# Decoder block with a mixture of experts: a new order behind the scan, earlier loads for the last group, and a second buffer for expert outputs

## The chip, the cores and the metric

One core of a Trainium2 chip runs the whole program. The metric is the device time of one execution in microseconds; the number given for a kernel is the median of several executions.

## What is computed

Eight rows (batch entries) of 256 positions with 256 features pass through a decoder block in float32. Each sublayer is added to its input and layer-normed:

```python
x = _layernorm(x + mamba_2_layers(x))      # selective scan, 512 channels x 64 states, 256 steps, twice
x = _layernorm(x + cross_attention(ctx, ctx, x))
# mixture of experts: 8 experts, hidden 1024, the best two of each position
gate_probs = softmax(xf @ gate_w.T); topk_scores, topk_idx = top_k(gate_probs, 2)
h   = relu(einsum('td,ehd->teh', xf, w1) + b1)
out = einsum('ted,te->td', einsum('teh,edh->ted', h, w2) + b2, combine)
x = _layernorm(x + out)
```

`combine` is zero but for the two chosen experts of a position, so only those two need be computed for it.

## The kernel before

**The scan.** There are 16 jobs (8 rows x 2 layers, `JOBS`, layer 1 of a row after layer 0 of the next row) and 64 states in each: 1024 steps (`STEPS`). A step is a scan over 128x1024 on VectorE (h), fed by a decay from ScalarE (dA), a product or a turned tile in PSUM (psX), and followed by a product on GpSimd (hC) and transposes that add up on TensorE (psY).

**Everything else is planned beside it.** `Schedule` builds three chains of small tasks: chain 0 is the work of the scan's own jobs (projections, convolution, residual and norm of a finished row), chain 1 is the attention and the gate of a row (`tasks_row`: x1_turn, q, score, prob, p_turn, av, o, resid2, norm2, x2_turn, logit, top, weights, count, place, list, send, b2, spill), chain 2 the experts (`tasks_experts`). A task has an engine, a nominal duration and what it needs. `fill` puts tasks between the scan's steps; `run_off` orders what is left behind the last step (`plan.tail`). Its rule: among the first `WINDOW` = 24 tasks of each chain whose needs are placed, the one with the earliest start is placed next, ties going to the lower chain. The result is one list, and every engine walks through its own pieces of that list in that order, waiting on semaphores. SyncE (SP) walks through it too: it issues the DMAs of the pieces, and a wait in one piece holds the pieces behind it.

**The experts.** The rows form four groups of two (`GROUPS`). When the last row of a group has been gated, `list` works out which expert each of the group's 15 tiles of 128 slots belongs to; four indirect DMAs per row (`send`, on GpSimd) put its positions into `x_slots` by slot. Tile t (0 to 59; 45 to 59 are the last group's, `TILE0[-2]` is 45) then runs:

- `tile_in`: SP waits and loads 128 rows of x and the expert's b1 (`load_tile`); for the first tile of a group it first waits until all sends of the group have landed, and behind x it asks for weights (`load_quarters`);
- `x_turn` (TensorE, transpose), `xg_copy` (ScalarE), 8 `hid` pieces (TensorE) with two `relu` (ScalarE), 8 `out` pieces (TensorE), `y_copy` into the single buffer yg (ScalarE), and `tile_out` (SP stores yg into `y_slots`).

An expert's weights come in four quarters, each a `w_up` and a `w_down` load of 256 KB. There are 3 slots of each during the scan and 9 behind it (`NW`, `NT`; the freed buffers of dA and h serve, so the trace calls these loads dA and h). `load_quarters` asks in turn for up and down loads until 9 quarters stand ahead of the pieces used; it is called at every second `hid` or `out` piece of the list, and it waits until the slot it fills is free. When the 15 tiles of a group are stored, each row fetches its two results per position (`fetch`, four indirect DMAs a row on GpSimd), adds them to its loaded accumulator (`acc_load`, `blend`), is normed (`bn3`, `rstd`, `norm3`) and stored; SP's store stands in the list at the place of `norm3`.

There is one `y_slots` tensor: the first `tile_out` of a group waits until the rows of the group before have been fetched. `x_slots` has two buffers. All these tensors are cleared during the first scan steps (`clear`, 24 DMAs of 512 KB, one every second step).

At the end of the scan in the kernel before, tiles 43 and 44 (third group), the fetches of rows 4 and 5, all of row 7 behind the scan, and the last group's 15 tiles are still to be done.

Of the kernel before, what the change touches and what calls it, by code (L numbers as in the profile page):

```python
# [20 lines left out]
P = 128  # L21
# [240 lines left out]

def tasks_experts(g):
    out = []
    for t in range(TILE0[g], TILE0[g + 1]):
        out.append(task("tile_in", t, 0, "DMA", 6000, ("list", GROUPS[g][-1], 0), ("sent", GROUPS[g][-1], 0),
                        *((("x_turn", t - 1, 0),) if t else ()), *((("y_copy", t - 2, 0),) if t > 1 else ())))
# [8 lines left out]
        for half in range(2):  # L276
            for i in range(4):
# [5 lines left out]
                     *((("fetched", GROUPS[g - 1][-1], 0),) if g and t == TILE0[g] else ()))]  # L283
# [20 lines left out]
class Schedule:  # L304
# [55 lines left out]
    def run_off(self, where, small, sums):  # L360
        banks = {"G": small, "M": sums}
        while any(self.chains):
            ready = []
            for rank, chain in enumerate(self.chains):
                for t in chain[:WINDOW]:
                    at, k = self.start(t, banks)
                    if at is not None:
                        ready.append((at, rank, chain, t, k))
            at, _, chain, t, k = min(ready, key=lambda r: r[:2])
            self.place(chain, t, at, k, where)  # L370
# [105 lines left out]
def decoder_block(nc, io, out):  # L476
    plan = Schedule()
    turn = plan.turn
    with ExitStack() as ctx:
# [127 lines left out]
        y_slots = nc.dram_tensor("y_slots", [SLOTS, D], F32, kind="Internal").ap()  # L607
# [37 lines left out]
        CLEARS = 3 * SLOTS * D // (P * KL * 2 * D)  # L645
# [8 lines left out]
        def _(eng):  # L654
# [8 lines left out]
            def clear(at):  # L663
                tensor, part = (*x_slots, y_slots)[at // (CLEARS // 3)], at % (CLEARS // 3)
                n = P * KL * 2
                on.wait_ge(got_cleared, 1)
                eng.dma_start(tensor[part * n:(part + 1) * n, :].rearrange("(p a) d -> p (a d)", p=P),
                              got[:, :, :, :].rearrange("p c k d -> p (c k d)")).then_inc(cleared, 16)
# [16 lines left out]
            def load_quarters(t):  # L685
                listed_to[0] = max(listed_to[0], PAIRS * TILE0[group_of_tile(t) + 1])
                missing = True
                while missing:
                    missing = False
                    for name, load in (("hid", load_up), ("out", load_down)):  # L690
                        if loaded[name] < min(used[name] + depth[0], listed_to[0]):
# [4 lines left out]
            def load_tile(t):  # L696
                g = group_of_tile(t)
                if t == TILE0[g]:
# [10 lines left out]
                if t == TILE0[g]:  # L709
                    load_quarters(t)  # L710

            def store_tile(t):
# [3 lines left out]
                for b in GROUPS[g - 1] if g else ():  # L716
                    on.wait_ge(fetched[b], 16 * 4)
                on.wait_ge(cleared, 16 * CLEARS)
                eng.dma_start(y_slots[bass.DynSlice(tile_combo(t) * P, P), :], yg[:, :]).then_inc(y_tile_out, 16)
# [110 lines left out]
        def _(eng):  # L830
# [13 lines left out]
            def small_work(pieces):  # L844
                for name, n, part in pieces:
# [25 lines left out]
                    elif name == "fetch":  # L871
# [6 lines left out]
                        eng.indirect_dma_start(got_of[n][:, tc, k, :], None, y_slots, bass.IndirectOffsetOnAxis(slot_of[:, n, k, tc:tc + 1], 0),  # L878
# [868 lines left out]
```

## Time and profile before

| | us |
|---|---|
| median of 3 runs (3365.19 to 3372.42) | 3367.84 |
| the profiled execution | 3358.99 |
| its span | 3357.3 |

| engine | busy us | share |
|---|---|---|
| PE (TensorE) | 2737.2 | 82% |
| DVE (VectorE) | 3050.3 | 91% |
| ACT (ScalarE) | 2743.0 | 82% |
| POOL (GpSimd) | 2658.3 | 79% |

DMA moved 319 MB, 95 GB/s over the span. In the slices of the page VectorE is at nine tenths or more nearly up to the last scan step at 3134 us and idle behind it; the DMA's rate goes up to three times its mean there. So a share over the whole span tells only of the scan; the 223 us behind it have to be read by themselves. Times in the rows are microseconds from the start of the span.

### The profile page before, as it was taken

The page shows a single profiled execution, that of the slowest core. Times are in us where ns is not written, and L with a number is a line of the kernel's source. Part 1 is how long each engine was busy: PE and PEld are TensorE (multiplying, and loading weights), DVE is VectorE, ACT ScalarE, POOL GpSimd, SP SyncE. Part 2 cuts the span into 40 slices and gives each one's busy share as a digit, 9 for nine tenths or more (in the row PEclk, how much of TensorE's full clock was granted, in tenths as well). Part 3 has the DMA queues.
Part 4 walks back from the last instruction along what each step waited for, and adds up shares of the span by engine and source line. Part 5 has one row for each costly group of instructions (what it writes and reads, how often), then busy time and mean ns, then how long its engine had stood idle before and what let it go on. Part 6 is the DMA issues. An engine that isn't in the chain of part 4 may idle for free.

```text
span 3357.3 us, 54622 instructions
## 1 busy us (share of the span) xinstructions
PE 2737.2 (82%) x19466; PEld 2406.5 (72%) x19466; DVE 3050.3 (91%) x2211; ACT 2743.0 (82%) x6424; POOL 2658.3 (79%) x1289
## 2 busy tenths in 40 slices
PE   6878787888878877888888888878888777888876
PEld 4767776777767766777776777767777666778665
DVE  6999999999999999999999999999999999999500
ACT  7889898898978898898989888897998869888422
POOL 5989998898989788887888788797887878877401
PEclk7999999999999999999999998999999979999988
DMA  3241111111111113223331333313232122433485
GB/s 100 96 147 58 45 54 52 45 55 45 49 60 45 46 45 119 89 77 117 102 115 60 114 123 112 129 68 125 96 102 93 50 86 82 149 122 129 133 284 187
DMA packets 151747, 319.34 MB, mean 95 GB/s; under 512 B 28570, under 2 KB 44963, under 8 KB 151092
## 3 DMA queue, kind: packets, MB, share of 16 engines
q1 hardware_dynamic: 147522, 305.08, 27.7%
q0 software_dynamic: 3072, 8.39, 0.7%
q8 instruction: 155, 2.54, 0.3%
q10 hardware_dynamic: 882, 2.38, 0.2%
q14 instruction: 116, 0.95, 0.1%
HBM read 285.90 MB, written 29.88 MB: 94 GB/s over the span
## 4 chain that ended last, share of the span: by engine, by line
DVE 28%; issue 28%; ACT 15%; PE 14%; POOL 13%; DMA 1%; SPq 1%; POOLq 0%; DVEq 0%
DVE h L1146 15%; POOL hC L916 12%; DVE psX L1136 10%; ACT dA L1114 7%; PE psY L1452 3%; PE psG L1399 3%; ACT xs L1085 3%; PE psX L1436 2%; PE psX L1434 1%; PE psX L1399 1%; PE psG L1478 1%; PE psX L1478 1%; ACT gT L965 1%; ACT diag_b L1083 1%; DVE gT L1161 0%
## 5 line engine op out<-in xcount | busy, mean ns | idle before, releaser
L916 POOL TENSOR_TENSOR hC<-h,cb 128x1024 f32<-128x1024 f32 x1024 | 2404.8, 2369 | 493.6 <-DVE h L1146 487.7
L1146 DVE TENSOR_TENSOR_SCAN h<-dA,psX 128x1024 f32<-128x1024 f32 (+1 forms) x1115 | 2305.6, 2102 | 70.1 <-PE psX L1436 34.1
L1114 ACT ACTIVATE dA<-dt,negA 128x255 f32<-128x255 f32 x4096 | 1716.5, 502 | 105.2 <-DVE h L1146 103.0
L1452 PE MATMUL psY<-ident,hC 128*128 128x128 f32 x8192 | 1123.5, 283 | 47.4 <-DVE gT L1161 37.3
L1452 PEld LDWEIGHTS psY<-ident,hC 128*128 128x128 f32 x8192 | 978.1, 146 | 61.7 <-DVE gT L1161 41.0
L1136 DVE TENSOR_TENSOR psX<-dtu,psX 128x1024 f32<-128x1024 f32 x513 | 619.6, 1208 | 9.5 <-PE psX L1423 9.3
L1436 PE MATMUL psX<-ident,xs 128*128 128x128 f32 x3280 | 465.0, 288 | 158.8 <-ACT xs L1085 78.2
L1085 ACT ACTIVATE xs<-dtuT,bT 128x512 f32<-128x512 f32 x820 | 545.9, 718 | 12.7 <-PE psX L1436 12.4
L1436 PEld LDWEIGHTS psX<-ident,xs 128*128 128x128 f32 x3280 | 387.2, 148 | 234.9 <-ACT xs L1085 151.4
L1423 PE MATMUL psX<-ident,bT 128*128 128x128 f32 x1026 | 217.3, 295 | 194.8 <-DVE h L1146 192.1
L1423 PEld LDWEIGHTS psX<-ident,bT 128*128 128x128 f32 x1026 | 117.4, 141 | 299.5 <-DVE h L1146 280.4
L1434 PE MATMUL psX<-diag_b,dtuT 128*128 128x128 f32 x1616 | 215.5, 289 | 63.3 <-DVE h L1146 38.9
L1434 PEld LDWEIGHTS psX<-diag_b,dtuT 128*128 128x128 f32 x1616 | 199.8, 201 | 84.0 <-issue 48.4
L1399 PE MATMUL psG<-xgT,w_up 128*128 128x128 f32 x1440 | 202.9, 285 | 12.4 <-DMA w_up<-in_w_exp 5.4
L1399 PEld LDWEIGHTS psG<-xgT,w_up 128*128 128x128 f32 x1440 | 186.9, 200 | 23.4 <-DMA w_up<-in_w_exp 6.9
L1478 PE MATMUL psG<-w_down,hid 128*128 128x256 f32 x720 | 193.5, 392 | 6.7 <-ACT hid L1066 4.7
L1066 ACT ACTIVATE hid<-psG,b_tile 128x128 f32<-128x128 f32 x388 | 109.3, 364 | 56.5 <-PE psG L1399 56.4
L1478 PEld LDWEIGHTS psG<-w_down,hid 128*128 128x128 f32 x720 | 127.9, 195 | 26.5 <-ACT hid L1066 8.2
L1358 DVE SCALAR_TENSOR_TENSOR acc<-got,slot_weight,acc 128x256 f32<-128x256 f32 x28 | 14.7, 543 | 144.4 <-DMA got<-y_slots,slot_of 124.7
L878 POOL DMA_INDIRECT got<-y_slots,slot_of x28 | 29.1, 1041 | 126.4 <-DMA y_slots<-yg 120.7
L1399 PE MATMUL psG<-xin,w_in 128*128 128x256 f32 x256 | 68.7, 399 | 8.8 <-DMA conv_w<-in_conv 6.2
L1083 ACT ACTIVATE diag_b<-ident,bT 128x128 f32<-128x128 f32 x202 | 69.3, 393 | 3.9 <-PE psX L1434 3.9
(206 smaller groups left out, 1992.7 us busy)
## 6 DMA issues: line engine op xcount, KB each, us to landing
cb<-c_dram SPq DMA_DIRECT2D x256, 512.0 KB
w_up<-in_w_exp SPq DMA_DIRECT2D x196, 256.0 KB, 3.0
w_down<-in_w_exp SPq DMA_DIRECT2D x196, 256.0 KB
dA<-in_w_exp SPq DMA_DIRECT2D x44, 256.0 KB, 4.4
h<-in_w_exp SPq DMA_DIRECT2D x44, 256.0 KB, 5.0
x_slots<-got SPq DMA_DIRECT2D x16, 512.0 KB, 5.3
xg<-x_slots SPq DMA_DIRECT2D x60, 128.0 KB, 2.7
y_slots<-yg SPq DMA_DIRECT2D x60, 128.0 KB
```

Source lines behind the costliest of these rows:

```text
L916: eng.tensor_tensor(hC[i % NHC][:, :, :], h[i % NH][:, :, :], cw.to_broadcast([P, KI, L]), ALU.mult).then_inc(times_c, 1)
L1066: made = eng.activation(hid[part][:, i, :], bank[k][:, i * P:(i + 1) * P], ACT.Relu, bias=b1_tile[n % 2][:, c:c + 1])
L1085: made = eng.activation(xs[:, tc, :], dtuT[n % 2][:, tc, :], ACT.Identity, scale=bT[n % 2][:, tc, s:s + 1])
L1114: made = eng.activation(dA[j % NA][:, c, 1:L], dt[n % 2][:, c, 1:L], ACT.Exp, scale=negA[:, JOBS[n][0], c, s:s + 1])
L1136: eng.tensor_tensor(x[:, :, :], dtu[n % 2][:, :, :], x[:, KI - 1:KI, :].to_broadcast([P, KI, L]), ALU.mult).then_inc(times_b, 1)
L1146: made = eng.tensor_tensor_scan(h[i % NH][:, part, :].rearrange("p c t -> p (c t)"), dA[i % NA][:, part, :].rearrange("p c t -> p (c t)"), ...
L1399: made = eng.matmul(dst, lhs, rhs, start=begin and i == 0, stop=end and i == len(terms) - 1)
L1423: made = eng.transpose(psX[i % 2][:, KI - 1, tc * P:(tc + 1) * P], bT[n % 2][:, tc, s:s + 1].to_broadcast([P, P]), ident[:, :])
L1434: made = eng.matmul(to, dtuT[i // S % 2][:, tc, c * P:(c + 1) * P], diag_b[:, tc, :], start=True, stop=True)
L1436: made = eng.transpose(to, xs[:, tc, c * P:(c + 1) * P], ident[:, :])
L1452: made = eng.matmul(psY[:, tc, c * P:(c + 1) * P], hC[i % NHC][:, c, tc * P:(tc + 1) * P], ident[:, :], start=s == 0 and c == 0, stop=s == ...
L1478: made = eng.matmul(bank[k][:, 0:D], hid[half][:, i, :], w_down[slot][:, i % 2, :], start=half == i == 0, stop=half == 1 and i == 3, skip_ ...
```

## The change

Five edits:

1. `run_off` looks at 48 tasks of each chain instead of 24, and orders PE and ACT tasks by their start plus 1500 ns for each rank of their chain (0, 1500, 3000); DMA, DVE and POOL tasks go by their plain start.
2. For the last group's tiles `tile_in` needs, in the plan, the x_turn and the second relu of the tile two before, in place of the x_turn of the tile before and the y_copy of the tile two before. The waits of `load_tile` itself are the same.
3. At the last group's first tile the weights of that tile alone (4 quarters, 8 loads) are asked for ahead of the wait for the sends; the call behind the load of x is dropped for this group.
4. `y_slots` has two buffers, used in turn; the first `tile_out` of a group waits for the fetches of the group before the last one, in the plan and in the code.
5. The clearing has 32 DMAs in place of 24.

```diff
+def tile_before(t):
+    if t >= TILE0[-2]:
+        return ("x_turn", t - 2, 0), ("relu", t - 2, 1)
+    return (*((("x_turn", t - 1, 0),) if t else ()), *((("y_copy", t - 2, 0),) if t > 1 else ()))
...
         out.append(task("tile_in", t, 0, "DMA", 6000, ("list", GROUPS[g][-1], 0), ("sent", GROUPS[g][-1], 0),
-                        *((("x_turn", t - 1, 0),) if t else ()), *((("y_copy", t - 2, 0),) if t > 1 else ())))
+                        *tile_before(t)))
...
                 task("tile_out", t, 0, "DMA", 2500, ("y_copy", t, 0),
-                     *((("fetched", GROUPS[g - 1][-1], 0),) if g and t == TILE0[g] else ()))]
+                     *((("fetched", GROUPS[g - 2][-1], 0),) if g > 1 and t == TILE0[g] else ()))]
...
-                for t in chain[:WINDOW]:
+                for t in chain[:2 * WINDOW]:
                     at, k = self.start(t, banks)
                     if at is not None:
-                        ready.append((at, rank, chain, t, k))
-            at, _, chain, t, k = min(ready, key=lambda r: r[:2])
+                        ready.append((at + (1500 * rank if t.eng in ("PE", "ACT") else 0), rank, chain, t, at, k))
+            _, _, chain, t, at, k = min(ready, key=lambda r: r[:2])
             self.place(chain, t, at, k, where)
...
-        CLEARS = 3 * SLOTS * D // (P * KL * 2 * D)
+        CLEARS = 4 * SLOTS * D // (P * KL * 2 * D)
...
-            def load_quarters(t):
+            def load_quarters(t, alone=False):
...
-                        if loaded[name] < min(used[name] + depth[0], listed_to[0]):
+                        if loaded[name] < min(used[name] + depth[0], PAIRS * (t + 1) if alone else listed_to[0]):
...
             def load_tile(t):
                 g = group_of_tile(t)
+                if t == TILE0[-2]:
+                    load_quarters(t, alone=True)
                 if t == TILE0[g]:
                     for b in GROUPS[g]:
                         on.wait_ge(sent[b], 16 * 4)
...
-                if t == TILE0[g]:
+                if t == TILE0[g] and t < TILE0[-2]:
                     load_quarters(t)
...
-                for b in GROUPS[g - 1] if g else ():
+                for b in GROUPS[g - 2] if g > 1 else ():
                     on.wait_ge(fetched[b], 16 * 4)
                 on.wait_ge(cleared, 16 * CLEARS)
-                eng.dma_start(y_slots[bass.DynSlice(tile_combo(t) * P, P), :], yg[:, :]).then_inc(y_tile_out, 16)
+                eng.dma_start(y_slots[g % 2][bass.DynSlice(tile_combo(t) * P, P), :], yg[:, :]).then_inc(y_tile_out, 16)
```

## Rows read from the trace of the kernel before

**Rows 1.** Stretches: us, PE, PEld, DVE, ACT, POOL busy (instructions), PE clock, DMA share, GB/s.
```profile
3150.00:3200.00 50.00, 29.53 (x148) 23.40 (x146) 15.95 (x65) 9.72 (x30) 14.33 (x15) 0.76 0.33 105
3200.00:3250.00 50.00, 41.70 (x239) 37.31 (x239) 3.98 (x11) 14.25 (x48) 0.72 (x1) 0.87 0.88 298
3250.00:3300.00 50.00, 46.82 (x310) 42.38 (x309) 0.00 (x0) 17.63 (x60) 0.00 (x0) 1.00 0.94 294
```

**Rows 2.** Timeline, row 7 behind the scan, in order of its chain: start, us, engine, line.
```profile
3142.40 1.04 PE L1558 MATMUL psX<-ident,gT 128*128 128x128 f32 x8
...
3155.69 0.47 ACT L939 ACTIVATE qT<-psX,b_att 128x256 f32<-128x256 f32 x1
3156.41 1.89 PE L1399 MATMUL psG<-kT,qT 128*128 128x256 f32 x8
3160.57 0.62 DVE L1263 TENSOR_SCALAR prob<-prob,small 128x256 f32<-128x256 f32 x2
3161.82 0.60 PE L1466 MATMUL psX<-ident,prob 128*128 128x128 f32 x4
3162.59 0.61 ACT L936 ACTIVATE x1T<-psX 128x512 f32<-128x512 f32 x1
3163.60 1.89 PE L1399 MATMUL psX<-x1T,vv 128*128 128x256 f32 x8
...
3185.08 0.17 DVE L1329 CAST slot_of<-small 128x4 int32<-128x4 f32 x1
```

**Rows 3.** Chain of waits that ended last, around the sends: start, us, what.
```profile
3190.05 2.39 DMA x_slots<-x,slot_of
...
3206.35 6.86 DMA xg<-x_slots
```

**Rows 4.** Timeline of SP's queue: start, us until issued, line, DMA.
```profile
3193.64 0.36 SPq L707 DMA_DIRECT2D xg<-x_slots  x1
...
3221.74 0.36 SPq L719 DMA_DIRECT2D y_slots<-yg  x1
```

**Rows 5.** Timeline, tiles 45 to 47, PE and ACT.
```profile
3196.70 0.69 PE L1655 MATMUL psX<-ident,xg 128*128 128x128 f32 x2 [9.67 <-DMA xg<-x_slots]
3199.44 2.05 PE L1399 MATMUL psG<-xgT,dA 128*128 128x128 f32 x8 [2.05 <-DMA dA<-in_w_exp]
3213.26 0.69 PE L1655 MATMUL psG<-ident,xg 128*128 128x128 f32 x2 [3.97 <-DMA xg<-x_slots]
3214.43 6.42 PE L1399 MATMUL psX<-xgT,dA 128*128 128x128 f32 x32 [0.47 <-ACT xgT L1054]
3220.69 3.62 PE L1478 MATMUL psG<-h,hid 128*128 128x256 f32 x16
3225.96 0.38 ACT L1073 ACTIVATE yg<-psG 128x256 f32<-128x256 f32 x1 [3.93 <-DMA y_slots<-yg]
3235.90 0.38 ACT L1073 ACTIVATE yg<-psX 128x256 f32<-128x256 f32 x1 [2.32 <-PE psX L1478]
```

**Rows 6.** The chain of waits in a later tile, and ACT's copy of the last one (timeline).
```profile
3248.49 3.47 PE psG L1478 x16
3251.98 0.26 ACT yg L1073
3252.26 0.39 ACT xgT L1054
...
3332.41 0.38 ACT L1073 ACTIVATE yg<-psX 128x256 f32<-128x256 f32 x1 [2.31 <-PE psX L1478]
```

**Rows 7.** Stretches of PE alone: us, PE busy (instructions), PE clock, DMA share, GB/s.
```profile
3206.00:3210.00 4.00, 3.29 (x16) 1.00 1.05 405
...
3216.00:3218.00 2.00, 2.00 (x12) 0.50 0.00 0
```

**Rows 8.** Stretches of the scan, with and without clears: columns as in rows 1.
```profile
100.00:400.00 300.00, 236.56 (x1846) 210.32 (x1846) 294.10 (x157) 263.72 (x616) 271.03 (x123) 0.98 0.28 92
400.00:700.00 300.00, 247.32 (x1844) 220.79 (x1845) 286.72 (x163) 262.68 (x609) 263.59 (x123) 0.95 0.14 50
```

More of the change, by code:

```diff
@@ L606, in decoder_block @@
         x_slots = [nc.dram_tensor(f"x_slots{i}", [SLOTS, D], F32, kind="Internal").ap() for i in range(2)]
-        y_slots = nc.dram_tensor("y_slots", [SLOTS, D], F32, kind="Internal").ap()
+        y_slots = [nc.dram_tensor(f"y_slots{i}", [SLOTS, D], F32, kind="Internal").ap() for i in range(2)]
         kept = nc.dram_tensor("kept", [ROWS, P, KL, D], F32, kind="Internal").ap()
@@ L663, in clear @@
             def clear(at):
-                tensor, part = (*x_slots, y_slots)[at // (CLEARS // 3)], at % (CLEARS // 3)
+                tensor, part = (*x_slots, *y_slots)[at // (CLEARS // 4)], at % (CLEARS // 4)
                 n = P * KL * 2
@@ L877, in small_work @@
                             on.wait_ge(blended, KL * n)
-                        eng.indirect_dma_start(got_of[n][:, tc, k, :], None, y_slots, bass.IndirectOffsetOnAxis(slot_of[:, n, k, tc:tc + 1], 0),
+                        eng.indirect_dma_start(got_of[n][:, tc, k, :], None, y_slots[GROUP_OF[n] % 2], bass.IndirectOffsetOnAxis(slot_of[:, n, k, tc:tc + 1], 0),
                                                bounds_check=SLOTS - 1, oob_is_err=False).then_inc(fetched[n], 16)
```

## Prediction

> **What bounds the kernel now.** I read the busy shares first, then the stretches behind the scan, then the chain of waits and the timelines of that part. The shares are the scan's: VectorE is the bound up to 3134 us, and nothing of the change enters a scan step but the clearing and small shifts of the plan. Behind the scan the stretches [rows 1] show two stages. Between 3150 and 3200 us no engine is the bound: TensorE is busy 29.5 of 50 us and DMA a third; it is a chain of small dependent steps of row 7, from the turn of its gated scan at 3142.40 to its slots at 3185.25 (3185.08 + 0.17) [rows 2]: 42.9 us. From 3200 us TensorE is the bound (41.7, then 46.8 of 50 us busy), with DMA busy 0.88 and 0.94 beside it. But that share is not a full queue: with the weights of 9 quarters asked for at once the same engines moved 405 GB/s [rows 7], against 294 in the steady stage [rows 1]. So there is room for an earlier burst.
>
> Between the two stages lies the join that the change aims at. The last send lands at 3192.44 [rows 3], 7.2 us behind the slots. SP loads the x of tile 45 at 3193.64 [rows 4], TensorE turns it at 3196.70, and then the first hid piece waits 2.05 us more, for weights, until 3199.44 [rows 5]. The x of tile 46 is issued at 3206.35, behind the 18 weight loads that one call of load_quarters makes, and takes 6.86 us [rows 3, 4]; TensorE idles 3.97 us for it and then runs at the lower clock: 32 matmuls of hid take 6.42 us [rows 5], at a granted clock of 0.50 [rows 7], where the 8.04 us tiles are at 1.00. y_copy of tile 46 then waits for yg to be stored: the store is issued at 3221.74, and the copy starts at 3225.96, 1.65 us behind the last matmul (3220.69 + 3.62 = 3224.31) [rows 4, 5]. Tile 47 is copied at 3235.90 [rows 5]. From there the tiles run evenly: 3235.90 to 3332.41 [rows 6] is 12 tiles of 8.04 us. Of each, 0.65 us are y_copy and xg_copy, with no matmul to cover them (0.26 + 0.39) [rows 6].
>
> **The plan, worked from its rule.** The planner's own nanoseconds serve for the order alone. *Row 7.* A tile piece (rank 2) is now placed ahead of a row piece (rank 1) only if it starts over 1500 ns before it. In the gap of resid1 to norm1 5 tile pieces of 520 fit, 4 in max to prob_norm, 5 in resid2 to norm2, 4 in the gate: 18 of the 32 of tiles 43 and 44. 14 come behind count, 3 of them ahead of w_turn. *SP.* tile_in 45 has its start at the landing of the sends; y_copy 44 starts a little earlier but carries +3000, so tile_in 45 stands ahead of tile_out 44, and SP is at load_quarters(45) when the list is made. tile_in 46 comes into the window of 48 as the last out piece of tile 44 is placed and goes right behind, ahead of all further weights. x_turn 46 then falls into the gap before tile 45's first hid. *Later tiles.* x_turn t+1 and out t have equal keys, the tie goes to the earlier task, so x_turn stays behind out and the exposed 0.65 us stays: I give nothing for the 13 even tiles, though tile_in is earlier. What hides this part of the change is that x is there in time already.
>
> **The sum, from the slots of row 7 (before: 3185.25, tile 47 copied 50.65 us later).**
> - Sends land after 7.2 us [rows 3]; 8 weight loads now go beside them. No row shows the two together. Bounds: 0 (the DMAs are busy 0.33 of this stage [rows 1]) and the 3.8 us by which the x load behind the burst was longer (6.86 against 3.06, 3193.64 to 3196.70) [rows 3 to 5]. The burst is 8 loads and not 18, and started earlier, so I take 0.7: 7.9.
> - x of tile 45, its b1, the spill of row 7 (it waits for b2_add, some 0.8 us, as the store of row 4 holds SP before) and x of tile 46: 46 is issued 2 us behind the sends and lands in 3.1 [rows 4, 5]: 13.0. x_turn 46 takes 0.7 at the low clock [rows 5]: the first hid at 13.7, against 14.2 before (3199.44). So x is nearly as late as before; the gain is that tile 46 is ready too.
> - Tile 45: TensorE has idled again, so I price it like tile 46 before, 6.42 + 3.62 less overlap = 10.1 (3214.43 to 3224.31 is 9.9 [rows 5]). If the clock stays up it is 7.3. Taken 10.1: 23.8.
> - Tile 46 without idle, waits or slow clock: 8.04 - 0.65 = 7.4; tile 47 an even 8.04: 39.2. Saved so far 50.65 - 39.2 = 11.4.
> - Row 7's chain itself. Waits of its pieces for tile pieces: score 0.25 (3156.16 to 3156.41), p_turn 0.63 (3161.19 to 3161.82), av 0.40 (3163.20 to 3163.60) [rows 2], and about 0.3 ahead of o. Saved 1.6, out of 42.9: the chain already runs nearly alone, and going first can give no more. TensorE now has pieces to do in the gate's gap, which may hold its clock: 0 to 2 more, not taken.
> - The stores of rows 4 and 5. Their fetches come behind the sends now, because tile 44 ends later; SP stands at the store of row 5 for some 8 us, and by my hand order tile_out 46 is just behind it (the two keys are 220 ns apart). yg is single, so y_copy 47 waits. Bounds: 0, and 4 us; the wait of this kind in the rows was 1.65 [rows 5]. Taken 2. The weights don't run out in it: 9 quarters are over two tiles, or 18 us.
> - Clears: 8 more of 512 KB. With the 24, VectorE was busy 294.1 of 300 us, without them 286.7 of 300 [rows 8]: nothing waits for them. Cost 0, bound 1 us. Second y buffer: before, nothing waited for it in the tail but SP at tile_out 45, when the fetches had landed; 0.
> - Behind the last y_copy (3332.41) all is as it was.
>
> Sum: 11.4 + 1.6 - 2.0 = **11 us**. On the profiled execution 3358.99 gives 3348.0; the median is 8.85 us above that execution, and I carry the saving over unchanged: 3367.84 - 11 = **3356.8 us**.
>
> **A rule that speaks against it.** The x of tile 46 took 6.86 us when weights were issued ahead of it, 3.06 us for tile 45 with none ahead [rows 3 to 5]. The Trainium skill, "DMA: Bandwidth & Descriptors", section "Queues, rings and completion order", says that each DMA engine consumes the descriptors of a ring in order. By that rule the early weights, now ahead of x 45, would hold it if they were still queued at the landing of the sends; the row on tile 46 agrees with it. At 405 GB/s [rows 7] 8 loads are 5.2 us, and the list is made about 6 us before the landing, so they should be just through.
>
> **Rivals.**
> 1. *The join costs less than I price:* TensorE's clock holds through the leftover pieces (tile 45 in 7.3, 2.8 saved), no wait for yg (2), the gate faster (1 to 2). Saves 15 to 18: 3350 to 3353. For it: 14 pieces lie in the join. Against: they end some 4 us before x lands, and after 3.97 us of idle the clock was at 0.50 [rows 5, 7].
> 2. *DMA and SP take it back:* the sends or x 45 wait for the weights (up to 3.8), y_copy waits 4, or tile_out 44 stands ahead of tile_in 45 after all, so that 8 loads at 0.52 us each of SP's time are ahead of x (4 us). 11 + 2 - 4 - 4 = 5 saved: 3363; or it doesn't reach the stage at all, 0: 3368.
> 3. *The scan's written order shifts, and it is slower.* In the plan of before, the first tile_out of the second group was held by the fetch of row 1; without that need tile pieces of group 2 may fall into other steps for some 200 steps, where each late piece holds VectorE. It decides from 18 us, 0.09 us a step: then +7 over before, 3375. For it: VectorE is at 98% there [rows 8], so nothing absorbs a piece in the wrong step. Against: y_copy 16, the next that needs the store, is planned 11 us later by other needs, so I expect the order to fall back within a few steps.
>
> **How the numbers follow.** Forecast 0.50 (saves 7 to 15, its own range 3353 to 3361), rival 1 0.17, rival 2 0.24, rival 3 0.09. 0.2%, 6.7 us, is about what a measurement of this kernel can tell from no change. Faster: the forecast, rival 1, and a fifth of rival 2: 0.72. Same: most of rival 2, 0.18. Slower: 0.10. The range leaves out rival 3 and the ends of 1 and 2: 3347 to 3366.
>
> **What would show it.** In the changed profile 8 weight loads are issued before the last send lands; two x loads stand together on SP; the first hid follows the landing by about 6 us; tile 46 follows tile 45 with no xg_copy wait; later tiles are 8.04 us apart; row 7's chain is 41 to 42 us. Wrong would be: a first hid later than 14.2 us behind the slots; an even stage other than 8.04; a wait of yg over 4 us; a scan that ends elsewhere than within 3 us of 3134; a chain of row 7 longer than before, because TensorE, given less to do in it, runs it at the low clock.

## The result, and the profile after

The changed kernel is slower: 3376.71 us median of 17 runs (3370.11 to 3384.75) against 3369.39 us for the kernel before (17 runs, 3364.36 to 3373.76) beside it, a ratio of 1.0024 (95% interval 1.0017 to 1.0030), or +7.3 us. The forecast was 3356.8 us in a range of 3347 to 3366, with 0.10 on slower: the sign was wrong, and the time lies above the range.

The profiled execution of after took 3382.01 us. The page's first part (busy time, share of the span, instructions of each engine):

```profile
span 3380.3 us, 54638 instructions
...
PE 2745.9 (81%) x19466; PEld 2413.6 (71%) x19466; DVE 3051.7 (90%) x2211; ACT 2744.5 (81%) x6424; POOL 2659.8 (79%) x1289
```

Same matmuls, same VectorE work, 16 instructions more in all than the 54622 before (the clears are 8 of them). Nothing in the totals tells where 7 us went, and the span of this execution is 23 us longer, not 7. So I looked first for the place from which two executions can be compared. Row 7's gated scan is turned at 3156.46 us here and at 3142.40 before [rows 2], 14.1 us later. In e1 below, whose scan has the same plan as after's, the same turn comes at 3145.9. VectorE's product of the first of the 16 jobs (gT) stands at 229.36 us in after and 225.76 in e1, that of the eighth at 1553.41 and 1551.49, that of the last at 3151.77 and 3141.29: the lead of e1 comes and goes by a few us along the scan. So this part of the difference is one between executions, and the following is measured from the turn, or from row 7's slots (the end of the CAST of slot_of), not from the start.

From the turn to the last y_copy it was 190.0 us before (3142.40 to 3332.41 [rows 2, 6]) and is 198.8 after: +8.8, against +7.3 in the medians. The loss is there, behind the scan. The stretches, with the columns of [rows 1]:

```profile
3150.00:3200.00 50.00, 38.78 (x193) 31.14 (x191) 14.52 (x59) 11.47 (x34) 2.89 (x4) 0.88 0.32 105
3200.00:3250.00 50.00, 32.34 (x163) 28.64 (x163) 6.48 (x16) 9.44 (x32) 11.90 (x13) 0.75 0.73 230
3250.00:3300.00 50.00, 43.83 (x276) 39.62 (x276) 2.42 (x8) 16.52 (x56) 0.71 (x1) 0.97 0.87 285
```

These stretches count from the start of the span, and row 7's slots come 12.9 us later here than before, so the lines can't be laid beside [rows 1] as they are. Over the stretch that lies behind the slots as 3200 to 3250 us does before (3212.92 to 3262.92) TensorE is busy 34.0 us instead of 41.7, at a clock of 0.83 instead of 0.87, while DMA moves 239 GB/s at a share of 0.76 instead of 298 at 0.88. TensorE, which sets the end here, stands still for longer, and over the stretch the DMA engines have room. In the 10 us in which it stands longest (3213 to 3223) they don't: there they are at 0.94 and 303 GB/s. So the thing to look for is not how much is moved, but in which order.

The timeline of PE and ACT at the join (start, us, engine, line; in brackets the idle time before and what ended it), to be read against [rows 2, 5]:

```profile
3156.46 1.04 PE L1567 MATMUL psX<-ident,gT 128*128 128x128 f32 x8
...
3198.00 0.17 DVE L1338 CAST slot_of<-small 128x4 int32<-128x4 f32 x1
...
3212.05 0.44 PE L1664 MATMUL psX<-ident,xg 128*128 128x128 f32 x2 [1.75 <-DMA xg<-x_slots]
3223.38 0.69 PE L1664 MATMUL psG<-ident,xg 128*128 128x128 f32 x2 [10.89 <-DMA xg<-x_slots]
3223.86 1.91 PE L1408 MATMUL psX<-xgT,dA 128*128 128x128 f32 x8
...
3233.52 0.38 ACT L1082 ACTIVATE yg<-psG 128x256 f32<-128x256 f32 x1 [2.08 <-PE psG L1487]
3236.89 3.62 PE L1487 MATMUL psG<-h,hid 128*128 128x256 f32 x16
3244.49 0.38 ACT L1082 ACTIVATE yg<-psG 128x256 f32<-128x256 f32 x1 [6.26 <-DMA y_slots<-yg]
3265.20 0.38 ACT L1082 ACTIVATE yg<-psX 128x256 f32<-128x256 f32 x1 [5.31 <-DMA y_slots<-yg]
...
3355.29 0.38 ACT L1082 ACTIVATE yg<-psX 128x256 f32<-128x256 f32 x1 [2.31 <-PE psX L1487]
```

Row 7's chain is 41.7 us (3156.46 to 3198.17), 1.1 shorter than before. Then the x of tile 45 is turned at 3212.05, and behind it the x of tile 46, for which TensorE stands idle 10.89 us. Tile 45's first hid comes behind that, at 3223.86, 25.7 us behind the slots instead of 14.2. Later two y_copies wait for the store of yg. ACT stands idle 6.26 and 5.31 us ahead of them, but part of that is the time of the matmuls (2.31 us in an even tile, as in the last row): behind the last matmul of their tile they wait 4.0 us (3236.89 + 3.62 = 3240.51 to 3244.49) and 3.0 us.

SP's queue in the same stretch (start, us until issued, line, DMA), against [rows 4]:

```profile
3200.16 0.33 SPq L747 DMA_DIRECT2D dA<-in_w_exp  x1
...
3203.79 0.54 SPq L761 DMA_DIRECT2D w_down<-in_w_exp  x1
3210.11 0.33 SPq L716 DMA_DIRECT2D xg<-x_slots  x1
...
3211.50 0.33 SPq L747 DMA_DIRECT2D dA<-in_w_exp  x1
...
3216.48 1.13 SPq L761 DMA_DIRECT2D h<-in_w_exp  x2
3217.80 0.33 SPq L716 DMA_DIRECT2D xg<-x_slots  x1
...
3218.91 0.61 SPq L728 DMA_DIRECT2D y_slots<-yg  x1
...
3233.16 1.87 SPq L761 DMA_DIRECT2D w_down<-in_w_exp  x2
3239.57 0.35 SPq L810 DMA_DIRECT2D y<-acc  x1
...
3240.64 0.35 SPq L728 DMA_DIRECT2D y_slots<-yg  x1
```

The 8 early weight loads go out at 3200.16 to 3203.79, as meant. But between the x of tile 45 (3210.11) and that of tile 46 (3217.80) stand 10 more weight loads, which I had not seen coming. The kernel before has 18 in that place, from the call in tile_in 45 that the change drops, and its x of tile 46 is issued 21.1 us behind the slots (3206.35) against 19.6 here: so late an x of tile 46 is not new, but before it only tile 46 waited for it. Further down the yg of tile 45, full at 3233.90, is stored at 3240.64 only: SP stood from 3235 to 3239.57 at the store of row 4 (L810), and tile_out is behind that in its queue.

The chain of waits around the sends, against [rows 3]:

```profile
3202.97 6.93 DMA x_slots<-x,slot_of
...
3218.91 4.83 DMA y_slots<-yg
3228.53 4.32 DMA got<-y_slots,slot_of
...
3240.64 3.77 DMA y_slots<-yg
```

The last send takes 6.93 us instead of 2.39, and the sends are through 11.7 us behind the slots instead of 7.2. The other rows are the second part: tile 44's y is stored at 3218.91, behind x of tile 46, so the fetch of row 4 starts at 3228.53 and row 4's store at 3239.57.

### The profile page after: what moved, and what is told of

Read it like the earlier page. It is cut to its first block, busy times and chain, and to the rows that moved or that the text cites. A ratio compares the mean times of both kernels' runs of the same rounds, so it can differ in the third digit from the quotient of the medians.

```text
span 3380.3 us, 54638 instructions
## 1 busy us (share of the span) xinstructions
PE 2745.9 (81%) x19466; PEld 2413.6 (71%) x19466; DVE 3051.7 (90%) x2211; ACT 2744.5 (81%) x6424; POOL 2659.8 (79%) x1289
## 4 chain that ended last, share of the span: by engine, by line
DVE 28%; issue 25%; ACT 17%; PE 16%; POOL 12%; DMA 1%; SPq 1%; POOLq 0%; DVEq 0%; ACTq 0%
DVE h L1155 14%; POOL hC L925 10%; DVE psX L1145 10%; ACT dA L1123 8%; PE psY L1461 4%; PE psG L1408 4%; ACT xs L1094 3%; PE psX L1445 2%; PE psX L1443 2%; PE psX L1408 1%; PE psG L1487 1%; PE psX L1487 1%; ACT gT L974 1%; ACT diag_b L1092 1%; DVE gT L1170 1%
## 5 line engine op out<-in xcount | busy, mean ns | idle before, releaser
L1155 DVE TENSOR_TENSOR_SCAN h<-dA,psX 128x1024 f32<-128x1024 f32 (+1 forms) x1115 | 2306.2, 2101 | 72.6 <-PE psX L1445 35.8
L1094 ACT ACTIVATE xs<-dtuT,bT 128x512 f32<-128x512 f32 x820 | 545.8, 718 | 14.4 <-PE psX L1445 14.0
L1443 PE MATMUL psX<-diag_b,dtuT 128*128 128x128 f32 x1616 | 215.6, 290 | 65.8 <-DVE h L1155 39.4
L1367 DVE SCALAR_TENSOR_TENSOR acc<-got,slot_weight,acc 128x256 f32<-128x256 f32 x28 | 14.8, 545 | 143.3 <-DMA got<-y_slots,slot_of 133.9
L887 POOL DMA_INDIRECT got<-y_slots,slot_of x28 | 29.1, 1040 | 137.7 <-DMA y_slots<-yg 126.2
L1408 PE MATMUL psG<-xin,w_in 128*128 128x256 f32 x256 | 69.1, 401 | 10.1 <-DMA conv_w<-in_conv 6.5
```

The costliest lines, as they stand in the source:

```text
L1094: made = eng.activation(xs[:, tc, :], dtuT[n % 2][:, tc, :], ACT.Identity, scale=bT[n % 2][:, tc, s:s + 1])
L1155: made = eng.tensor_tensor_scan(h[i % NH][:, part, :].rearrange("p c t -> p (c t)"), dA[i % NA][:, part, :].rearrange("p c t -> p (c t)"), ...
L1408: made = eng.matmul(dst, lhs, rhs, start=begin and i == 0, stop=end and i == len(terms) - 1)
L1443: made = eng.matmul(to, dtuT[i // S % 2][:, tc, c * P:(c + 1) * P], diag_b[:, tc, :], start=True, stop=True)
```

## The experiments

The theory after reading: (A) the early call of load_quarters raises listed_to to the whole last group, so that every later piece that has used up a quarter (here the out pieces of tile 44, which stand between tile_in 45 and tile_in 46 in SP's list) asks for further weights at once, ahead of x 46. Rivals: (B) the order by rank itself: tile 44 ends later, and with it the rows 4 and 5 whose fetches, loads and stores SP works through in the same queue; (C) the early weights delay the sends; (D) the second buffer or the clears cost time in the scan. One table for all runs. The columns from "sends landed" to "last" (the y_copy of tile 59) give us behind row 7's slots, each from one profiled execution. "Sends landed" is taken at the first instruction that the landing lets go, up to 0.1 us behind the landing itself:

| kernel | median us (runs), kernel before beside it | ratio (95%) | turn to slots | sends landed | first hid of 45 | y_copies of 45, 46, 47, 48, 49 | last | turn to last |
|---|---|---|---|---|---|---|---|---|
| before | 3369.4 (17) | | 42.8 | 7.3 | 14.2 | 24.1, 40.7, 50.7, 58.7, 66.7 | 147.2 | 190.0 |
| after | 3376.7 (17), 3369.4 | 1.0024 (1.0017 to 1.0030) | 41.7 | 11.8 | 25.7 | 35.3, 46.3, 56.0, 67.0, 76.7 | 157.1 | 198.8 |
| e1_listed | 3367.6 (12), 3369.5 | 0.9999 (0.9986 to 1.0012) | 40.2 | 11.2 | 15.5 | 22.8, 38.8, 49.1, 59.4, 69.1 | 149.5 | 189.8 |
| e2_no_early | 3373.3 (12) | 1.0017 (1.0004 to 1.0030) | 39.4 | 7.2 | 26.4 | 35.8, 46.7, 56.3, 66.3, 74.4 | 154.8 | 194.2 |
| e3_order_only | 3374.2 (12) | 1.0015 (1.0004 to 1.0027) | 39.4 | 7.3 | 11.8 | 25.3, 50.1, 55.4, 65.4, 74.0 | 154.4 | 193.8 |
| e4_buffers_only | 3370.3 (12) | 1.0003 (0.9993 to 1.0014) | 42.8 | 7.3 | 13.3 | 23.3, 40.9, 50.8 | 147.3 | 190.1 |
| e6_no_rank | 3362.7 (12), 3370.3 | 0.9981 (0.9972 to 0.9990) | 42.8 | 7.3 | 19.7 | 29.3, 36.3, 44.3, 52.4 | 140.9 | 183.7 |
| e7_x_first | 3374.6 (12) | 1.0013 (1.0004 to 1.0022) | 40.8 | 7.3 | 13.6 | 27.2, 46.6, 56.7, 65.9, 73.9 | 154.3 | 195.1 |
| e8_no_rank_x_first | 3373.1 (12) | 1.0010 (1.0000 to 1.0021) | 42.8 | 7.3 | 14.4 | 25.2, 45.6, 56.3, 64.3 | 152.8 | 195.6 |
| e9_turn_ahead | 3361.4 (8) | 0.9975 (0.9964 to 0.9985) | 42.1 | 7.3 | 14.8 | 26.9, 44.7, 51.1, 58.3, 65.5 | 137.8 | 179.9 |
| e10_pool_store_ahead | 3352.7 (6), 3370.0 | 0.9946 (0.9934 to 0.9958) | 42.8 | 7.3 | 14.4 | 25.4, 37.6, 45.0, 52.3 | 131.8 | 174.6 |
| e11_pool_store | 3365.1 (11), 3370.0 | 0.9986 (0.9976 to 0.9996) | 41.7 | 11.2 | 15.5 | 22.8, 33.9, 47.3, 58.3, 66.4 | 146.8 | 188.5 |
| e12_turn_ahead_alone | 3370.3 (11), 3370.0 | 0.9997 (0.9988 to 1.0005) | 42.1 | 7.3 | 13.2 | 31.9, 43.8, 51.2, 61.4, 69.9 | 149.2 | 191.3 |
| e13_turn_ahead_early_x | 3361.4 (9), 3369.1 | 0.9968 (0.9957 to 0.9979) | 42.8 | 7.3 | 27.4 | 36.5, 43.7, 51.0, 58.2 | 137.7 | 180.6 |

The last column and the ratio mostly go together. Executions of one kernel differ by 3 to 18 us, and the last column comes from a single one of them, so it tells where time goes rather than how much by 1 or 2 us.

### The early call without its side effect (e1_listed)

```diff
             def load_quarters(t, alone=False):
-                listed_to[0] = max(listed_to[0], PAIRS * TILE0[group_of_tile(t) + 1])
+                if not alone:
+                    listed_to[0] = max(listed_to[0], PAIRS * TILE0[group_of_tile(t) + 1])
```

> The changed kernel with one line mended: the early call at tile 45 no longer raises the bound on which quarters may be loaded, so the out pieces of tile 44 behind it in the list ask for no weights, and the x of tile 46 is issued right behind the spill of row 7. Theory A (the loss is at the join: x of tile 46 stands behind 10 weight loads, and x_turn 46, placed ahead of tile 45's first hid, holds TensorE for it): the x of tile 46 lands within 6 us of the sends, the first hid of tile 45 starts about 16 us behind the slots of row 7 (25.7 in the changed kernel, 14.2 in the one before), the last y_copy comes 138 to 147 us behind the slots (157.1 and 147.2), and the time is 3362 to 3368 against about 3369 of before. Rival B (the scan is slower, through its own written order and the 8 clears): the time stays at about 3377.

Measured: 3367.56 us, ratio 0.9999, and 189.8 us from turn to last copy against 198.8. SP's queue in e1:

```profile
3197.45 0.33 SPq L717 DMA_DIRECT2D xg<-x_slots  x1
...
3199.36 0.33 SPq L717 DMA_DIRECT2D xg<-x_slots  x1
...
3200.91 0.33 SPq L748 DMA_DIRECT2D dA<-in_w_exp  x1
...
3212.52 0.85 SPq L762 DMA_DIRECT2D w_down<-in_w_exp  x2
3220.38 0.35 SPq L811 DMA_DIRECT2D y<-acc  x1
...
3221.43 0.36 SPq L729 DMA_DIRECT2D y_slots<-yg  x1
```

Now the two x loads stand together, 1.9 us apart, as I had forecast for after, and the weights come behind them. The first hid is at +15.5 instead of +25.7. (A) is shown: one line was worth 8 to 9 us. What is left: y_copy 46 waits, as the timeline of ACT shows:

```profile
3208.92 0.38 ACT L1083 ACTIVATE yg<-psG 128x256 f32<-128x256 f32 x1 [2.31 <-PE psG L1488]
3224.97 0.38 ACT L1083 ACTIVATE yg<-psG 128x256 f32<-128x256 f32 x1 [11.34 <-DMA y_slots<-yg]
```

yg is full at 3209.30, and its store is issued at 3221.43, behind row 4's store at 3220.38 at which SP had stood since 3213.4. Tile 45 is copied 12.5 us earlier than in after (22.8 against 35.3), tile 46 only 7.5 us earlier (38.8 against 46.3): the rest is lost here. So the one line takes the kernel from slower to level with the kernel before, and the 11 us of the forecast still don't come.

### The edits by themselves (e2_no_early, e3_order_only, e4_buffers_only)

e2 is after without the early call:

```diff
-                if t == TILE0[-2]:
-                    load_quarters(t, alone=True)
...
-                if t == TILE0[g] and t < TILE0[-2]:
+                if t == TILE0[g]:
```

> The changed kernel without the early weights: they are asked for behind the x of tile 45 again, 9 quarters at once. Tells apart what the early weights cost the sends. If the sends land late because of the weights, they land 7 us behind the slots of row 7 here (11.8 in the changed kernel). Theory A says that the whole doesn't gain by it: the x of tile 46 now stands behind 18 loads, the first hid starts 22 to 26 us behind the slots, and the time is within 3 us of the changed kernel's 3377. If the early weights were the main loss, the time would be 5 us or more below it.

e3 is the kernel before with edit 1 alone, the lines of run_off (48 tasks, 1500 ns for each rank); e4 is it with edits 4 and 5 alone (y_slots twice, 32 clears, the wait for the group before the last one).

> The kernel before with the new rule of run_off alone (48 tasks, rank weights). Row 7's chain is 41 to 42 us long instead of 42.9. Tile 44 ends later, so the fetches of rows 4 and 5 come later; with one y_slots tensor the first tile_out of the last group waits for them on SP, and y_copy 46 behind it. Theory A: 3 to 8 us slower than before (3372 to 3377), the whole difference behind the first hid of tile 45. If going first is what pays, 1 to 2 us faster than before.

> The kernel before with the second y_slots buffer, its need two groups back and the 8 more clears alone. The plan inside the scan differs from before in three steps as in the changed kernel, and the part behind the scan is that of before but for the order that follows from the dropped need. Rival B: slower by 5 to 8 us, as the changed kernel. Theory A: within 3 us of before.

Measured: 1.0017, 1.0015 and 1.0003. (D) falls: with the second buffer and the clears the time can't be told from that before, and from turn to last copy it is 190.1 us against 190.0. The start of row 7's turn doesn't follow the clears either: 3142.4, 3144.5, 3153.7 and 3154.7 us in the four profiles with 24 of them (before, e12, e3, e13), 3145.5 to 3156.5 in those with 32. VectorE in the scan's stretch with clears, as in [rows 8], in e4:

```profile
100.00:400.00 300.00, 237.81 (x1836) 213.27 (x1834) 291.22 (x155) 261.30 (x611) 269.05 (x122) 0.97 0.31 104
```

The order by rank costs by itself, 4.7 us in the medians: in e3 row 7's chain gains 3.4 us (39.4), twice what I gave it, and the tiles lose 7.2 (147.2 to 154.4 from the slots). The chain was worth more than I said and its price, of which I had 2 us, was larger still.

e2 shows what edit 2 does without the early weights. Timeline of PE, tile 46's x behind the 18 weight loads of tile_in 45:

```profile
3211.33 0.69 PE L1662 MATMUL psG<-ident,xg 128*128 128x128 f32 x2 [15.87 <-DMA xg<-x_slots]
```

x_turn 46 is now planned ahead of tile 45's hid, and so the first hid waits for an x that isn't needed until a tile later: +26.4. Before, the same late x of tile 46 cost 3.97 us of idle time [rows 5], since tile 45 ran in front of it. (C): with the early loads the sends take 11.2 to 11.8 us, without them 7.2 to 7.3 in every kernel of the table. It is there, about 4 us, above the upper bound that I had set.

### The order by rank taken out (e6_no_rank)

```diff
-                        ready.append((at + (1500 * rank if t.eng in ("PE", "ACT") else 0), rank, chain, t, at, k))
+                        ready.append((at, rank, chain, t, at, k))
```

This on top of e1.

> e1_listed without the rank weights: run_off goes by the plain start again (48 tasks stay). Tests the second loss: with the rank weights tile 44 ends behind row 7, so the fetches of rows 4 and 5 come late, SP stands at their stores, tile_out stands behind them and y_copy waits for yg (in e1_listed tiles 46 to 49 take 15 us more than 8.04 each). Theory A: row 7's chain goes back to 42.8 us (+2.6), the waits for yg go, tile 47 is copied about 38 us behind the slots (49.1 in e1_listed), the last tile at 135 to 138 (149.5), and the time is 3355 to 3361. If going first were worth more than it costs, the time would be above that of e1_listed (3367).

Measured: 3362.74 us, 0.9981, the first kernel that is faster than before, 4.8 us under e1 (and 1.7 us above what was expected). Row 7's chain is back at 42.8 (2.6 lost) and the tiles gain 8.6 (149.5 to 140.9). With e3 this shows (B): what the last row's chain gains by going first, the left-over tiles and the rows that hang on them lose twice over (e3) or more (e6). The factor isn't a fixed price: between e7 and e8 below, which differ by the same line, there are 1.5 us in the medians and -0.5 us from turn to last. And part of e6's time is an accident: SP stood at row 4's store, so the "early" weights were asked for only as the sends had landed, and beside no send:

```profile
3197.50 0.34 SPq L811 DMA_DIRECT2D y<-acc  x1
3198.39 0.35 SPq L748 DMA_DIRECT2D dA<-in_w_exp  x1
...
3203.27 0.33 SPq L717 DMA_DIRECT2D xg<-x_slots  x1
```

The first hid is thereby later than in e1 (+19.7), and still the end is earlier: row 4's store and row 5's load of acc (issued at 3205.76) were both ahead of the next 10 weight loads (from 3206.81).

### x ahead of the weights (e7_x_first, e8_no_rank_x_first): both forecasts missed

To have neither the slow sends nor a late x, e7 takes e1 and asks for no weights before both x's:

```diff
-                if t == TILE0[-2]:
-                    load_quarters(t, alone=True)
...
-                if t == TILE0[g] and t < TILE0[-2]:
+                if t == TILE0[g] and t < TILE0[-2] or t == TILE0[-2] + 1:
                     load_quarters(t)
```

e8 is the same on e6.

> e1_listed with the weights of the last group asked for behind the x of tiles 45 and 46 and not ahead of the sends. The sends land 7.2 us behind the slots (11.2 in e1_listed: the price of 8 weight loads beside them). Theory A: the first hid comes 12 to 14 us behind the slots (15.5) although its weights are asked for later, the waits for yg stay, and the time is 1 to 4 us below e1_listed. If early weights are worth having, the first hid is later than in e1_listed.

> Both: plain start and x of tiles 45 and 46 ahead of the weights. If the two losses are separate, both gains add: sends landed at 7.2 us, first hid at 12 to 14, last tile copied 132 to 136 us behind the slots, time 3352 to 3358.

Measured: 3374.63 and 3373.14 us, 7 and 10 us above the kernels that they are made from. The join is as expected (sends 7.3, first hid +13.6 and +14.4). What I had not priced is what the burst of 18 weight loads now stands ahead of. SP's queue in e8:

```profile
3212.78 0.39 SPq L806 DMA_DIRECT2D acc<-kept  x1
...
3225.76 0.35 SPq L809 DMA_DIRECT2D y<-acc  x1
...
3228.49 0.33 SPq L715 DMA_DIRECT2D xg<-x_slots  x1
```

and who waits for it, VectorE and TensorE:

```profile
3220.68 1.92 DVE L1366 SCALAR_TENSOR_TENSOR acc<-got,slot_weight,acc 128x256 f32<-128x256 f32 x4 [20.88 <-DMA acc<-kept]
...
3232.18 0.69 PE L1663 MATMUL psX<-ident,xg 128*128 128x128 f32 x2 [8.19 <-DMA xg<-x_slots]
```

The load of acc for row 5 is behind the burst, in time of issue and in the DMA queues, so row 5 is blended at 3220.68; its store goes out at 3225.76; x of tile 47 is in the list behind that store, and TensorE idles 8.19 us for it. The store of tile 45's yg is issued behind that x, at 3231.58, so ACT stands 15.74 us ahead of y_copy 46. In e7, where tile 44 ends late, the store of row 4 is issued at 3234.91 only, and ACT stands 16.93 us ahead of y_copy 46. It is the loss of after once more, moved by one tile: a step with nothing to do with experts (the end of row 5) holds the tiles since both are in one in-order queue.

### Which of SP's waits to move (e9 to e13)

Two remedies follow. One takes the stores of rows 4 and 5 out of SP's queue and has GpSimd issue them, with a semaphore of their own (e11 on e1, e10 on e9):

```diff
-                    elif name == "norm3":
+                    elif name == "norm3" and n not in (4, 5):
...
+                    elif name == "norm3" and n in (4, 5):
+                        on.wait_ge(normed[2], n + 1)
+                        eng.dma_start(out[n], acc_of[n]).then_inc(y_pool, 16)
```

The other removes what I had left alone in the prediction, the 0.65 us in each tile in which no matmul covers y_copy and xg_copy: in the last group's task list tile_in, x_turn and xg_copy of a tile go ahead of the second half of the out pieces of the tile before (e9 on e8, e12 on the kernel before, e13 on e12 with edit 2 added):

```diff
+    if g == len(GROUPS) - 1:
+        for t in range(TILE0[g] + 1, TILE0[g + 1]):
+            mine = [x for x in out if x.piece in (("tile_in", t, 0), ("x_turn", t, 0), ("xg_copy", t, 0))]
+            out = [x for x in out if x not in mine]
+            at = next(i for i, x in enumerate(out) if x.piece == ("out", t - 1, (1, 0)))
+            out[at:at] = mine
```

> e8_no_rank_x_first, and in the last group tile_in, x_turn and xg_copy of a tile stand ahead of the second half of the out pieces of the tile before. Tests that the 8.04 us of an even tile are bound by TensorE and the 0.65 us of y_copy and xg_copy that nothing covers: then a tile takes 7.3 to 7.6 us, with DMA at 310 to 320 GB/s, and the time is 6 to 10 us below e8_no_rank_x_first. If DMA were the bound behind it (busy 0.93 in the even tiles), a tile would stay at 8 us.

> e9_turn_ahead with the stores of rows 4 and 5 issued by GpSimd behind its rstd, not by SP. In e8 and e9 SP stood at the store of row 5 for some 11 us, with the x of tile 47 behind it (that tile's x_turn came 40 us behind the slots). If the wait in SP's queue is the cause, tile 47's x_turn comes 28 to 33 us behind the slots, the last y_copy 126 to 131 us (137.8), and the time is 7 to 12 us below e9_turn_ahead: 3350 to 3355. If it is the late landing of data, nothing changes.

> e1_listed with the same move of the two stores to GpSimd, and nothing else. Isolates the second loss of the changed kernel: in e1_listed the copies of tiles 45 to 49 are 16.0, 10.3, 10.3 and 9.7 us apart and not 8.04, 15 us in all. If SP standing at the stores is the cause, 6 to 12 of the 15 us go (SP still waits at the accumulator load of row 5 for the first store's landing) and the time is 3356 to 3362. If it is tile 44 ending late by itself, the distances stay.

> The kernel before with one change of the plan: in the last group tile_in, x_turn and xg_copy of a tile stand ahead of the second half of the out pieces of the tile before. None of the changed kernel's five edits. Expected: the even tiles take 7.2 us (7.25 in e9_turn_ahead) in place of 8.04, 13 tiles give 10 us, the join stays as before, time 3358 to 3362. If the gain of e9 hangs on the earlier join, the time is within 3 us of before.

> e12_turn_ahead_alone with the changed kernel's needs of tile_in for the last group (edit 2), and nothing else of it. Two questions. The x loads: in e12 they came too late for an earlier x_turn (12.7 us of waits for xg, tiles of 7.4 to 10 us); if edit 2 mends that, the tiles take 7.25 us here. The join: x_turn 46 is planned ahead of tile 45's first hid and x of tile 46 stands behind 18 weight loads, as in e2_no_early; if that order alone is the first loss, the first hid starts 24 to 28 us behind the slots although there are no early weights and no rank weights. Together: last y_copy 138 to 144 us behind the slots, time 3360 to 3367. If edit 2 doesn't matter, the time is that of before.

Measured: e9 3361.38 us (12 under e8, where 6 to 10 were expected), e10 3352.74 us, 0.9946 (0.9934 to 0.9958) and 17 us under the kernel before, the best of all. The stretch of 3260 to 3300 us (columns of [rows 1]) in e9 and in e12:

```profile
3260.00:3300.00 40.00, 40.00 (x274) 37.34 (x273) 0.00 (x0) 16.44 (x54) 0.00 (x0) 1.00 0.99 330
```

```profile
3260.00:3300.00 40.00, 36.19 (x242) 32.48 (x242) 0.00 (x0) 14.75 (x49) 0.00 (x0) 1.00 0.87 279
```

With x turned early TensorE is busy 40.00 of 40 us and a tile takes 7.25 us instead of 8.04. In e12 it is the same order but for the time at which x is asked for: tile_in still needs x_turn of the tile before and y_copy of the one two before in the plan, and so x comes late. Timeline of PE in e12:

```profile
3228.52 0.44 PE L1661 MATMUL psX<-ident,xg 128*128 128x128 f32 x2 [3.68 <-DMA xg<-x_slots]
...
3245.80 0.44 PE L1661 MATMUL psX<-ident,xg 128*128 128x128 f32 x2 [2.42 <-DMA xg<-x_slots]
```

Behind tile 46 seven such waits of TensorE sum up to 11.6 us and eat the gain: 0.9997, a miss for the 8 to 12 us that I had expected. e13 adds edit 2 and nothing else, and the tiles run at 7.25 us from tile 46 on, though the first hid is as late as in e2 (+27.4): 0.9968. So edit 2, which gave nothing as long as x_turn stood behind out, is what makes that move pay.

e11 was a miss in size. Tiles 46 to 49 of e1 take 14 us more than 8.04 each (22.8 to 69.1), and of these I expected 6 to 12 back and got 2 to 3 (146.8 against 149.5 from the slots, 2.4 in the medians). SP's queue in e11 tells why:

```profile
3217.74 0.85 SPq L748 DMA_DIRECT2D dA<-in_w_exp  x2
3226.54 0.33 SPq L809 DMA_DIRECT2D acc<-kept  x1
```

The store is gone from the queue, and SP stands at the next step of the same kind, the load of acc for row 5, from 3218.6 to 3226.54; y_copies of tiles 47 and 48 are late instead of that of 46 (the wait of 46 is 6.43 us now, 11.34 before). In e10 the same edit gave 6.0 us from the slots (137.8 to 131.8) and 8.6 in the median, since there SP doesn't stand at that load. SP's queue in e9, row 5's store and x of tile 47, and then that x in e10 (row 7's slots are at 3197.43 and 3198.17 us):

```profile
3230.82 0.35 SPq L815 DMA_DIRECT2D y<-acc  x1
...
3233.55 0.33 SPq L721 DMA_DIRECT2D xg<-x_slots  x1
```

```profile
3223.91 0.33 SPq L721 DMA_DIRECT2D xg<-x_slots  x1
```

The same load is asked for 25.7 us behind the slots instead of 36.1, since no store is ahead of it that waits.

## Why the prediction was wrong, point by point

- **Sends beside the early weights: 0.7 taken, bound 3.8; it was 4.5** (11.7 against 7.2), 3.9 in e1. I called the bound generous because the burst is 8 loads and not 18, and taken at the landing they should have been "just through". The row on tile 46's x (6.86 us behind a burst) [rows 3] had the right size, and I put my value near the other end, by the share of 0.33, a mean over a stage that says nothing of the few us in question: from 1 us behind the slots to the landing it was 0.19 (75 GB/s) before and 0.68 (238 GB/s) in after.
- **"tile_in 46 ... goes right behind, ahead of all further weights": wrong, and the step that sets the sign.** The list of SP was as I had worked it out: tile_in 45, the pieces of tile 44, tile_in 46. I overlooked that pieces of tile 44 also call load_quarters, and that the early call had lifted their limit. Ten loads went between the x's; x 46 was issued 19.6 us behind the slots and not 10, about as late as before (21.1), and took 5.6 us. First hid: 13.7 forecast, 25.7 measured; e1 with the one line mended 15.5, of which 3.9 are the sends. That line was worth some 8 of the 18 us between forecast and result: 9.1 in the medians, 7.6 from the slots to the last copy. With it mended the kernel is level with the one before, and the slower sends and the waits for yg keep the gain away. I had named "a first hid later than 14.2 us" as the sign of an error.
- **x_turn 46 ahead of tile 45's first hid: right in the order, wrong in the price.** I took it as the gain ("tile 46 is ready too"); the same order makes the first hid wait for whatever is late in the second x. e2 shows this without early weights, 12 us later than before (26.4 against 14.2), and e13 without the order by rank too (27.4).
- **Tiles 45 and 46: 10.1 and 7.4 forecast.** Tile 45 took 9.7 (3223.86 to 3233.52), right. Tile 46 was to follow without idle and took 11.0 (its y_copy 35.3 to 46.3), the wait for yg in it. Before, it took 16.6; this gain of 5.6 us came.
- **The stores of rows 4 and 5: 2 taken, bound 4; it was much more.** Tile 44 is later by the rank order and its y_out stood behind x 46; rows 4 and 5 follow, and SP stands at them with tile_out behind. The y_copies of tiles 46 and 48 wait 4.0 and 3.0 us behind their last matmul, and behind each of these two waits TensorE starts the next tile at the lower clock. PE alone in after (us, busy, granted clock, DMA share, GB/s), behind the two waits and in an even tile:

```profile
3245.40:3248.40 3.00, 3.00 (x16) 0.53 1.10 362
3266.00:3269.00 3.00, 3.00 (x15) 0.51 0.97 351
3284.00:3287.00 3.00, 3.00 (x30) 1.00 0.82 239
```

  At 0.51 to 0.53 (1.2 GHz) it starts half as many matmuls as at 1.00 (2.4 GHz): tiles 47 and 49 took 9.67 us instead of 8.04, 3.3 us together. With the waits that is 10 us, against the 2 taken. The part of the clock I had left out. I had found the place and the mechanism, and had sized it from the one small wait of before (1.65 us [rows 5]), when the tile ahead of it was on time.
- **Row 7's chain: 1.6 forecast; 1.1 in after and e11, 2.0 in e7, 2.6 in e1, 3.4 in e2 and e3.** Right in sign, and of the right size. How much it is hangs on the clock: after, e11 and e1 run the same 154 matmuls in it, in 41.7, 41.7 and 40.2 us at granted clocks of 0.87, 0.87 and 0.96; e7, e2 and e3 run 160, in 40.8, 39.4 and 39.4 us at 0.92, 0.96 and 0.96. Before it was 0.89: the clock in after was hardly lower, and the chain was shorter all the same. But that going first "can give no more" than 1.6 was wrong by up to 1.8 us. It doesn't pay for the delay of the tiles (e6).
- **Even tiles 8.04, second buffer 0, clears 0: right** (nine tiles from 84.7 to 157.1 after; e4 190.1 against 190.0). Rival 3, the only case that I had on the slower side, didn't come about: its mechanism is excluded by e4. Slower it became by the mechanisms of rival 2, which I had let end at 0 saved: I added its parts up to 8 us, and 18 were lost on the forecast.
- **The rule of the Trainium skill** that was weighed, in-order consumption of a ring ("DMA: Bandwidth & Descriptors", "Queues, rings and completion order"): the x of tile 46 took 5.6 us behind 10 weight loads (3217.80 to 3223.38), and in e2 6.3 us behind 18 (3205.04 to 3211.33; the 15.87 us for which TensorE stood are for the larger part the late issue). By that rule the burst spoke against the change, and these rows agree with it. I dismissed it for x 45, rightly (issued at 3210.11, turned at 3212.05), and didn't ask the same of x 46.

The bookkeeping from the slots, after against before: first hid +11.5, of it 4.5 the sends and the rest the 10 loads and the x behind them; tiles 45 and 47 -0.3 each; tile 46 -5.6; tiles 48 and 49 +4.6 (the wait of 3.0 and the lower clock); sum +9.9, as at the last copy; chain of row 7 -1.1: +8.8, against +7.3 in the medians.

Open: a second yg buffer, which would take the stores' wait away from y_copy directly, wasn't tried, and so no run separates the wait for yg from the late refills of weights that share SP's queue. What in the loads slows the sends isn't settled either, nor why the clock in row 7's chain was 0.87 in two executions and 0.96 in a third under the same plan.

## What to carry to other kernels

When a step is moved forward in a queue, list what each later entry of that queue will do under the new state, with the limits and counters that the moved step raises, not only where the entries stand: here the whole sign hung on one counter that a helper raised as a side effect. On an in-order queue that serves two chains, price a delay of the one by what stands behind its next waiting entry for the other, and put stores that wait on slow chains on another engine's queue once nothing else of that chain waits there too (1 to 3 us while a second wait stood behind, 5 to 9 us when not). Covering an operation that had no cover in each of the even tiles (0.65 us each) gave more (12 us in e9) than mending the one join (9 us in e1), and an early load pays only together with the order that can use it.

## What the runs showed of the hardware

- Eight weight loads (2 MB) on SP's queue, issued while four indirect sends of GpSimd are being made, stretch the last send from 2.39 to 6.93 us and the landing of all four from 7.2 or 7.3 us (before and the ten kernels without such loads) to 11.2 to 11.8 us (after, e1, e11), while the DMA share from just behind the slots to the landing is 0.68 (238 GB/s) in after and 0.19 (75 GB/s) before. The DMA engines were not full, and the sends were slower all the same.
- A DMA share of 0.94 at 294 GB/s [rows 1] was no limit: in tiles of 7.25 us the same engines moved 330 to 334 GB/s at a share of 0.99, with TensorE busy all the time.
- In after TensorE was at 0.53 and 0.51 of its clock behind idle times of 4.47 and 3.53 us, in the kernel before at 0.50 behind 3.97; the next tile took 9.67 us instead of 8.04, so that the wait of 3.0 us for yg cost 4.6. It is not so every time: in e12 the clock was 1.00 right behind an idle time of 3.68 us (3228.50 to 3230.00).
- Executions under the same scan plan can be 10 us apart at its end: the turn of row 7 came at 3145.9 us in e1 and at 3156.5 in after.
- The same list of 154 matmuls in row 7's chain took 40.2 us at a granted clock of 0.96 and 41.7 at 0.87.
